# The last unit's values of each attention group are done behind the first scores of the next group

## What is computed

```python
x = x + _L0_attn_a_ref(_layernorm(x), Wq, Wc, Wk, Wv, Wo)      # full attention, rotary positions
x = x + _L0_ffn_ref(_layernorm(x), ...)
x = x + _L0_attn_b_ref(_layernorm(x), w_attn, ...)             # causal attention, alibi bias
x = x + _L0_ffn_ref(_layernorm(x), ...)

# both attentions, 32 heads of 16 features:
scores = einsum('bqhd,bkhd->bhqk', q, k) * scale               # b: + bias, -inf above the diagonal
probs = softmax(scores, axis=-1)
attn = einsum('bhqk,bkhd->bqhd', probs, v)
```

## Time and profile before

| | us |
|---|---|
| median of 3 runs | 1784.81 (1781.09 to 1786.96) |
| the profiled execution | 1787.05 |
| its span, first to last instruction | 1785.2 |
| busy: PE / DVE / ACT | 1646.3 / 1393.8 / 971.8 |

### The profile page before, as it was taken

The page is one execution under the profiler, slowest core; times in us unless marked ns, Lnnn a source line. Parts: engine busy times, 40 slices in busy tenths (PEclk is TensorE's granted clock), DMA queues, the critical chain, the costliest instruction groups (busy, mean ns, idle before and its releaser), DMA issues. The chain is left out here.

```text
span 1785.2 us, 32918 instructions
## 1 busy us (share of the span) xinstructions
PE 1646.3 (92%) x13040; PEld 849.3 (48%) x13040; DVE 1393.8 (78%) x3007; ACT 971.8 (54%) x1103; POOL 138.6 (8%) x216
## 2 busy tenths in 40 slices
PE   6898999999999999999879999899999999999598
PEld 3554333333333333333335777555454545454476
DVE  3766799999999999999366364568888888885486
ACT  3432277777777777777711112126666666667110
POOL 3332200000000000000000011010000000003000
PEclk9999699999999999999999999989999999999799
DMA  7766334333333332330260433663636363632311
GB/s 217 226 165 193 81 56 85 63 62 64 60 63 65 55 55 56 56 55 12 86 196 1 141 116 104 202 155 57 118 73 103 65 109 60 108 61 63 103 71 71
DMA packets 116801, 167.58 MB, mean 94 GB/s; under 512 B 20772, under 2 KB 58036, under 8 KB 116532
## 3 DMA queue, kind: packets, MB, share of 16 engines
q1 hardware_dynamic: 115176, 160.99, 39.1%
q0 software_dynamic: 1472, 4.49, 1.3%
HBM read 100.41 MB, written 64.50 MB: 92 GB/s over the span
## 5 line engine op out<-in xcount | busy, mean ns | idle before, releaser
L356 DVE TENSOR_REDUCE mxp<-ps_m 128x1 f32<-128x512 f32 x1280 | 799.3, 684 | 69.3 <-PE ps_m L322 63.6
L673 ACT ACTIVATE a_p<-a_ps_s 128x1024 f32<-128x1024 f32 x512 | 522.2, 1025 | 149.8 <-PE a_ps_s L594 138.4
L673 ACT ACTIVATE b_p<-b_ps_s 128x1024 f32<-128x1024 f32 (+1 forms) x320 | 294.7, 938 | 157.9 <-PE b_ps_s L594 154.6
L353 DVE CUSTOM_DVE_ANT_0 ps_m<-ps_m,b_masks 128x128 f32<-128x128 f32 (+3 forms) x512 | 240.1, 517 | 45.1 <-PE ps_m L322 40.9
L322 PE MATMUL ps_m<-slot_qk 62*128 62x512 f32 (+3 forms) x624 | 230.7, 451 | 12.4 <-DVE mxp L356 9.0
L322 PE MATMUL ps_m<-a_slot_qk 62*128 62x512 f32 x640 | 238.1, 450 | 0.8
L594 PE MATMUL a_ps_s<-a_slot_qk 64*128 64x512 f32 x640 | 232.2, 443 | 1.3
L618 PE MATMUL a_ps_o<-a_p,a_slot_v 128*32 128x256 f32 x2560 | 205.6, 390 | 10.0 <-ACT a_p L673 5.4
L594 PEld LDWEIGHTS a_ps_s<-a_slot_qk 64*128 64x128 f32 x640 | 96.2, 185 | 128.8 <-issue 122.7
L594 PE MATMUL a_ps_s<-slot_qk 64*128 64x512 f32 x384 | 136.3, 455 | 0.6
L618 PE MATMUL a_ps_o<-a_p,slot_memory 128*32 128x256 f32 x1536 | 124.3, 393 | 7.4 <-ACT a_p L673 3.3
(11 more groups left out here) (205 smaller groups left out, 2343.7 us busy)
## 6 DMA issues: line engine op xcount, KB each, us to landing
va_groups<-w_o SPq DMA_DIRECT2D x16, 512.0 KB, 3.7
ka_parts<-pa_parts SPq DMA_DIRECT2D x16, 512.0 KB, 3.8
qa_parts<-pa_parts SPq DMA_DIRECT2D x32, 256.0 KB, 3.7
kb_parts<-slot_memory SPq DMA_DIRECT2D x16, 512.0 KB, 4.1
qb_parts<-slot_memory SPq DMA_DIRECT2D x32, 256.0 KB, 3.8
vb_groups<-w_proj SPq DMA_DIRECT2D x16, 512.0 KB, 3.4
a_slot_qk<-qa_parts SPq DMA_DIRECT2D x60, 128.0 KB, 4.1
a_slot_qk<-ka_parts SPq DMA_DIRECT2D x48, 128.0 KB, 6.3
```

The source lines that it names most:

```text
L353: dve.tensor_tensor_reduce(from_, from_, mask_of_query[:, CHUNK - keys:], 1.0, LOWEST, ALU.add, ALU.max, accum_out=to).then_inc(piece_take ...
L356: dve.tensor_reduce(to, from_, AX.X, ALU.max).then_inc(piece_taken, 1)
L673: act.activation(p_sb[:, (2 * u + pair) % NP, :, off:CHUNK], ps_s[:, 2 * pair:2 * pair + 2, off:CHUNK], ACT.Exp, scale=scale).then_inc(exp ...
```

## The change

`values` of the last unit is no longer called at the end of `step`. A new helper `values_behind` calls, behind the scores of unit 0 of group s, the values of the last unit of group s-1 (nothing for s = 0), and for every other unit what was called before. After the last group both parts are called once. ScalarE's `copy_out` of a group's second half moves behind both exponentials of unit 0 of the next group; for the last group it is called after the loop. Nothing is added or taken away, on no engine.

```diff
--- before.py
+++ after.py
@@ -622,6 +622,13 @@
                     if part:
                         mm.then_inc(pv_done, 1)
 
+                def values_behind(s, u, part):
+
+                    if u:
+                        values(s, s % SLOTS, u - 1, part)
+                    elif s:
+                        values(s - 1, (s - 1) % SLOTS, NU - 1, part)
+
                 def half_unit(s, j, u, pair, lo, hi):
 
                     scores(s, j, u, pair, 0)
@@ -634,14 +641,11 @@
                     for u in range(NU):
                         lo, hi = AHEAD + before_unit[u], AHEAD + before_unit[u + 1]
                         cut = lo + PAIR * ((hi - lo + PAIR) // (2 * PAIR))
+
                         half_unit(s, j, u, 0, lo, cut)
-                        if u:
-                            values(s, j, u - 1, 0)
+                        values_behind(s, u, 0)
                         half_unit(s, j, u, 1, cut, hi)
-                        if u:
-                            values(s, j, u - 1, 1)
-                    values(s, j, NU - 1, 0)
-                    values(s, j, NU - 1, 1)
+                        values_behind(s, u, 1)
 
                 def keep_clock(columns):
 
@@ -654,6 +658,8 @@
                     keep_clock(CHUNK // 2)
                 for s in range(NG):
                     step(s, s % SLOTS)
+                for part in range(2):
+                    values_behind(NG, 0, part)
 
             @block.scalar
             def _(act):
@@ -675,11 +681,13 @@
                                            scale=scale).then_inc(exp_done, 1)
                         if u == last_of[0] + 1:
                             copy_out(s, 0)
-                    copy_out(s, 1)
+                        if u == 0 and s:
+                            copy_out(s - 1, 1)
 
                 early.stores.wait(act, B)
                 for s in range(NG):
                     step(s)
+                copy_out(NG - 1, 1)
 
             @block.vector
             def _(dve):
```

## The result

The changed kernel takes **1796.53 us**, median of 4 runs (1794.54 to 1798.13), against 1784.47 for the kernel before (4 runs): ratio 1.0068, 95% interval 1.0047 to 1.0089. It is slower by 0.7%. The forecast was 1782.5 with a range of 1767 to 1790, and no change as the likeliest: it was wrong. The profiled execution took 1795.21 us with a span of 1793.4, where the forecast for it was 1784.8 and the one before took 1787.05.

A forecast was written before the change was run, and what follows sets the result against it. Both attentions were taken as set by TensorE's queue, VectorE close behind. -13.0 (a) + 10.7 (b) = -2.3 us gave 1784.8 for the profiled execution, and 1782.5 as median (2.2 below it), range 1767 to 1790.

The forecast's parts named there:

- The gain in a: Attention a, group boundaries: 4.22 us instead of 5.09, 0.87 us at each of 15, 13.0 us gained.
- Rivals 2 and 4: Attention a: copy's wait hidden, 1774.5 us, chance 0.08; or VectorE is the bound, nothing won, 1795.5 us, chance 0.05.
- barely: Attention a: VectorE takes 1.20 us for a half-unit's two pieces against TensorE's 1.23, so it follows.
- The mechanism of the loss in b: Attention b: later copy delays SP's stores and the maxima rows behind them, unit 3 waits; 10.7 us lost in sum.
- The middle taken for the DMA's time: Attention b, maxima rows: DMA time between 2.2 and 2.9 us from the first issue, taken as 2.6.
- The third group: Attention b: rows issued 2.5 us later meet the end of a large load; 0 to 2.5, taken as 0.3 us.
- The last: Attention b, last group: no pieces, copy some 2.2 us later, 1637.3 against 1635.39, 1.9 us lost.
- 2.50 after the copy's end: SP's queue in attention b: maxima rows issued 2.50 us after the copy's end, behind five stores, at 1312.7.
- Rival 3: Attention b: stores issue more slowly at their new place, rows 1.1 us later, 15 x 1.1 = 17: 1799.5 us, chance 0.10.
- I go by the rows: TensorE's clock: longer pauses than 0.19 us in attention a left it alone, so the new wait costs nothing.
- Rival 5: TensorE's clock falls at attention b's waits, 2.05 us a stretch, one in every group 31 us: 1813 us, chance 0.03.
- The rule that was weighed: TensorE's clock: short idles between groups of products, often enough, make it swing between two levels; by it 1813 us.

The follow-up runs named there:

- b alone: The new order in attention b only, attention a as in the kernel before: 1806.82 us, ratio 1.0138 against the kernel before.
- a alone: The new order in attention a only, attention b as in the kernel before: 1773.11 us, ratio 0.9945 against the kernel before.
- rows first: Changed kernel, but in attention b SP issues the second half's maxima rows before the previous group's stores: 1769.78 us, ratio 0.9916 against the kernel before.
- five spare DMAs: Kernel before plus five useless small DMAs on SP ahead of the maxima rows in attention b: 1812.1 us, ratio 1.0165.

## Why the prediction was wrong

**The gain in a was right**, term by term: 1.24 for each half-unit up to V(15,1), then 1.76 with 0.45 of waiting, VectorE no longer starved, 12.6 us where 13.0 were forecast. Rivals 2 and 4 are out. The condition, that VectorE would follow "barely", held.

**The mechanism of the loss in b was right, and so was the regular size.** V(0,0) came 0.27 earlier in the kernel without the late rows, unit 3 waits 0.77 to 0.80 in the regular groups (0.9 were forecast), and five groups in a row repeat in 29.87 to 29.91, against 29.30 before: 0.58 a boundary, forecast 0.65. The copy came 2.46 later (2.5 were forecast), and V(0,0) follows it, as forecast: it starts 0.15 behind the copy's end, as it does in the middle of a group of a, where the view names the copy as what it waited for. Here TensorE is idle for only 0.14 before it, and the view names no wait that short. The middle taken for the DMA's time, 2.6 us, was right too: the rows issued at 1303.46 let unit 3 start at 1306.09, 2.63 later. The third group (0.3 forecast) lost nothing (29.90 before, 29.95 after). The last (1.9 forecast) waited 1.41 us; it is 3.9 longer from copy to copy (27.44 before, 31.29 after), but much of that is the low stretch that began at 1610.8 and reached into it. With b alone, where the lower clock takes 2 us of it and not 6, it is 1.7 longer.

**The first step that failed: SP's issue times were taken from one boundary and held constant.** "2.50 after the copy's end" rests on one boundary. The same distance is longer in several groups of both kernels, since some single stores take 0.7 to 1.8 us to issue and not 0.42. The view of the tile had it, in the spread of one line of the kernel before (least, median, most in ns):

```profile
L525 SPq DMA_DIRECT2D ob_sums<-out_b_sums x128: 310/421/1661, 1200.7 to 1655.0; - x128
```

and so had SP's timeline of before, at a boundary that I did not read:

```profile
1425.50 2.93 SPq L525 DMA_DIRECT2D ob_sums<-out_b_sums  x4
```

There the rows were 1.1 us later than at 1310.18, and no one waited, because 1.9 us of room hid it. The change used up that room, and from then on every slow issue was a wait of TensorE. The 15 regular waits would be 15 x 0.78 = 11.7; they were 18.2. Of the other 6.5 us, **5.9 us** are this, and 0.6 is the last group, whose stores were not slow.

Rival 3 had the price of slow issues right (1.1 us) and their number wrong: it put them in all 15 groups, and got 0.10. But the place does matter. Where the stores stand as before, the rows are late by more than 0.5 us in the 9th and 11th groups, in the kernel before and in a alone. Where they wait for the later copy, it is five groups in the changed kernel and the same five and one more in b alone. So the spread of before, put into the sum, would have given some 2 us (1.1 and 0.9) and not 5.9; rival 3 had a third of its groups right.

**The second step that failed: the clock.** "I go by the rows" compared waits of 0.19 and 0.54 us with one of 0.9, and found that the clock had not fallen at any of them. That is still true: no wait below 1.3 us was followed by a fall. But the waits did not stay at 0.9, they reached 2.15 through the first step, and behind the three longest the clock fell, for 27.3 us. The price, by the lengths, is at most **9.9 us**. The three groups with a fall show 9.1 of it directly. One of them runs between these two copies:

```profile
1265.90 0.59 ACT L670 ACTIVATE out_b_sums<-b_ps_o 128x512 f32<-128x512 f32 x1
...
1300.38 0.59 ACT L670 ACTIVATE out_b_sums<-b_ps_o 128x512 f32<-128x512 f32 x1
```

That is 34.48 us, against 29.03 for the same group with the rows first. The wait of 2.15 is in it and 3.3 are left; in the other two 2.5 and 3.3 are left. The twelve groups without a fall are each 0.04 to 0.08 longer than their wait explains, and that is most of the remaining 0.8. The counts give somewhat more: at the pace of the stretch ahead of the first fall (900 products in 88.90 us) the 57, 47 and 57 products of the low stretches take 5.6, 4.6 and 5.6, against 10.2, 6.9 and 10.2; that is 11.4, an estimate, since some records may be missing. Per fall the prediction had 2.05, less than the 2.5 to 3.3 here, since two of the three stretches were longer than the one read. Rival 5 was priced for every group; it came in three, and got 0.03.

```profile
1184.00:1272.90 88.90, 81.63 (x900) 42.78 (x900) 75.46 (x245) 56.71 (x64) 2.85 (x11) 1.00 0.43 80
```

The rule that was weighed, of the Trainium skill, TensorE: Matmul & The Clock Gate, section "A second HAM failure mode: psum-queue depth-cycling", speaks of a clock that swings where short idles recur. What the runs show is another pattern: waits of 0.8 in group after group leave the clock at 1.00, and single long ones are followed by a fall.

**The sum as it should have been**, for b: 448.6 is the length without waits, 4.2 below that of before; + 11.7 regular waits + 5.9 slow issues + 0.6 more in the last group + 9.9 clock = 476.7. The last term is what is left over, so that the sum comes out proves nothing; the 9.1 above is its check. The prediction had 452.8 + 10.7 = 463.5. Against 1784.8 for the profiled execution, b accounts for +13.2, a for +0.4 and the part ahead of the first copy and between the two for -3.2: 1795.2.

**The range** ended at 1790 because rivals 3, 4 and 5, at 0.18 together, were left outside it, and 3 and 5 were priced each by itself. In the kernel the one feeds the other: the slow issues made the waits behind which the clock fell.

## What to carry to other kernels

When a producer on a shared DMA queue comes later, what is behind it on the queue loses its room, so read the room first, and then read the whole spread of the queue's issue times against it, not one boundary. Even that spread is only that of the old place: here the slow issues were in two groups of 15 before and in five after. Issue the transfer that the critical engine needs next ahead of stores that wait for something and that nobody needs soon: in this kernel moving one call on SP turned a change that costs 0.7% into one that gains 0.8%. And a wait that is short in most groups and long in some is priced twice, by itself and by what TensorE's clock does behind the long ones.

## What the runs showed of the chip that was not expected

**In attention b, where TensorE is busy 91 to 93% of the time, every wait of 1.73 us and more was followed by a fall of the clock.** In the three kernels with late rows (the changed one, b alone, five spare DMAs) there are 45 waits of unit 3. All 13 of 1.73 us and more have a stretch at 0.50 that begins in the last 0.4 us of the wait or up to 1.8 us behind it; of the six from 1.30 to 1.62 one has (1.41 us, in b alone), the others not; of the 26 up to 1.18 none. No stretch at 0.50 in b begins elsewhere in these kernels, and with TensorE kept busy for part of the wait there was none. The stretches last 3.4 to 13.7 us. In all of b the busy share is still 440.2 of 476.0, so the mean tells nothing of it.

**Issuing a small DMA on SP is not of constant cost.** A store of 32 KB (L525, b) takes 0.42 us to issue by the median and up to 2.1. In five runs (before, after, a alone, b alone, rows first) 38 of the 39 such stores of 0.7 us and more were issued while a packet of the queues of kind "instruction" was moving, against 63 of the 601 shorter ones. The DMA view of 1265 to 1271 us of the changed kernel, with the longest four of its stores (queue, kind, packets, MB, share):

```profile
q1 hardware_dynamic: 118, 0.13, 8.8%
q8 instruction: 1, 0.02, 1.5%
q14 instruction: 1, 0.01, 0.5%
```

Such packets also move while issues are of ordinary length, and no experiment moved them, so this is a coincidence in time and not a shown cause. The slow issues stood in the same groups in two pairs of kernels (above), which fits something tied to the place in the program better than chance; what it is stays open. That the DMA of the rows is not what varies is shown: from the issue of the first of the two to the landing of the last it took 2.57 to 2.61 us in every group of the changed kernel's b.
